# A decoder layer on one core: attention rounds written out, context products dealt unevenly over them, weight scaling moved ahead

## The chip, the core and the metric

One core of a Trainium2 chip runs the whole program. The metric is the device time of one execution in microseconds; the median of three runs is given. Matmuls run on PE (TensorE); DVE is VectorE, ACT is ScalarE, POOL is GpSimd, and SP is the engine whose queue issues nearly all DMAs.

## What is computed

The reference is one decoder layer on x of shape (16, 256, 512), cut here to its three steps:

```python
x = x + attn(layernorm(x))       # 16 heads of 32, causal softmax, biased q, k, v, o
x = x + xattn(ctx, ctx, layernorm(x), ssm_kernel, D, 8)
                                 # kv = k_i * v_j products, causal convolution with ssm_kernel, plus D*kv, times q
x = x + ffn(layernorm(x))        # rows of w_gate_up, w_down, x and h rounded to 255 levels of their maximum
```

Two preparations don't depend on x: the products kv of the context with itself (here called **context products**), and the rounding of the FFN weights by the largest magnitude of each row.

## The kernel before

**Two phases.** `attention` (L234) works through 16 batches in 16 rounds; `mixer` (L1006) then does the second and third step in rounds of its own. Engines run their own instruction streams in program order and meet at semaphores, so an engine that waits holds up everything behind the wait.

**A round** i is `body(i, p)` on every engine: 16 steps, one head each. PE at step s (L708) computes the scores of head s (L661), turns the probabilities of head s-2 (L670), does the round's share of the twelve `ROUND` jobs (L77), then multiplies the probabilities of head s-3 by the values (L685 to L687). The jobs are: projections of the next batch (QK at steps 0 to 7, V at 8 to 11), turning of the last batch's attention (A at 8 and 10) and of a normalised input (X at 12 and 13), and the output projection (O at 13 to 15). They share three PSUM banks: a job may begin once the job three before it is emptied. A job's bank is emptied by ACT one step after the job's last step (`high`, the fp16 part; for A it is L759), and then by DVE (`low`, the remainder; for A it is L882). ACT at step s (L823): such emptying, `prob_high` of head s-2 (L788), `exps` of head s (L780). DVE at step s (L963): every fourth step `divide` (L928, L932), then `maxima` of head s (L915), emptying, `prob_low` of head s-2 (L921), and at step 8 `row_stats` of batch i+2 (L897, L903). Rounds 0, 1, 14 and 15 are written out; rounds 2 to 13 are a hardware loop of two rounds an iteration (L733 on PE, L848, L989, L576, L484), six iterations.

**Context products.** 64 sets, four a round. A set is loaded by SP into one of two `c_in`, multiplied by POOL (`pairs`: L532 and L534, counted by `kv_made`), copied to fp16 by ACT (`pairs_high`, L794, counted by `kv_high`), its remainder is taken by POOL (`pairs_low`, L539, counted by `kv_low`), and SP stores it (`store_pairs`, L394), which `kv_stored` tells. ACT's copies stand behind `exps` of a step:

```python
PAIRS_HIGH = (8, 12, 15, 3)      # L91: steps of the copies of sets 0, 1, 2 of this round, and of set 3 of the round before
```

POOL's order in a round (L550) is fixed: value bias of the last four heads of the batch before (L523), bias of the residual (L557), products 0, low part of the last set of the round before, value bias, `norm(i + 2)`, products 1, low part 0, value bias, products 2, low part 1, value bias, products 3, low part 2. `norm` waits for DVE's `row_stats` of step 8:

```python
pool.wait_ge(stats_done, i + 1)  # L509, first line of norm; then L510 to L516
```

**Weight units.** `Weights` (L125): eleven units of two rows of tiles each for w_gate_up and four for w_down. SP loads a unit (L163, 512 KB), DVE finds the rows' maxima (`find_maxima`, L168) and from them scale and inverse (`find_scales`, L175 and L178), and ACT scales (`scale_rows`, L187). Units 0 to 3 are done in round 15 (`UNIT_MAX`, `UNIT_SCALE`, L87), 4 to 6 between the A and O jobs behind the rounds (L1000), 7 to 10 at the start of the mixer (L1743 to L1752, L1476, L1478 and `SCALE_AT`). PE turns them in the mixer (L194); the transposition of all scales (L1289) stands behind them and ahead of the first convolution (L1202).

Of the kernel before, what the change touches and what calls it, by code (L numbers as in the profile page):

```python
# [85 lines left out]
IN_ROUND, IN_TAIL = 4, 7  # L86
UNIT_MAX = {1: 0, 4: 1, 7: 2, 10: 3}  # L87
UNIT_SCALE = {3: 0, 6: 1, 9: 2, 12: 3}
JOBS_END = [("A", 0, -1, 0, 0), ("A", 1, -1, 0, 0), ("O", 0, -1, 0, 0), ("O", 1, -1, 0, 0)]
LOOP0, LOOP1 = 2, B - 2  # L90
PAIRS_HIGH = (8, 12, 15, 3)  # L91
# [142 lines left out]
def attention(nc, ctx, x, wqT, wkT, wvT, woT, bq, bk, bv, bo, w1, W, eye, mask, x1d, eye_f, eye_b, wqkv, x_all,  # L234
# [115 lines left out]
    with nc.Block() as block:  # L350
        @block.sync
        def _(sp):
# [30 lines left out]
            def load_ctx(i, k):  # L383

                alone(sp, started)
                reached(sp, kv_made, i * 4 + k - 1)
                sp.dma_start(c_in[k % 2][:], ctxr[bass.ds(i * 2 + k // 2, 1), :, PM * (k % 2):PM * (k % 2) + PM, :]
                             .rearrange("h p m c -> p (h m) c")).then_inc(ctx_in[k % 2], 16)

            def store_pairs(i, k):  # L390

                alone(sp, started)
                sp.wait_ge(kv_low, i * 4 + k + 1)
                sp.dma_start(kvd[bass.ds(i * 4 + k, 1)].rearrange("q p c -> p (q c)"),  # L394
                             kv_s[k % 2][:].rearrange("p a m c -> p (a m c)")).then_inc(kv_stored[k % 2], 16)
# [12 lines left out]
            load_ctx(0, 0)  # L408
            load_ctx(0, 1)
# [4 lines left out]
            def body(i, p):  # L414
# [25 lines left out]
                if isinstance(i, int) and i == B - 2:  # L440
# [1425 lines left out]
```

## Time and profile before

| | |
|---|---|
| median of 3 runs | 1227.86 us (1225.43 to 1227.94) |
| the profiled execution | 1225.79 us, of which the span of the instructions is 1224.0 us |
| busy share of the span: PE, DVE, ACT, POOL | 93%, 82%, 72%, 77% |
| attention rounds 2 to 13, by PE's scores of head 0 | 108.34 to 537.11 us |
| rounds 14 and 15 | 537.11 to 570.45 to 608.66 us |

All times below are counted from the first instruction. A round is cut where PE starts the scores of head 0. A row of a timeline reads: start, duration, engine, line, operation, output<-inputs, shapes, count, and in brackets the idle time of the engine before it with what ended it. "PEclk" is the granted TensorE clock as a share of 2.4 GHz; 0.50 is 1.2 GHz.

### The profile page before, as it was taken

How to read it: one execution, taken by the hardware profiler on the slowest of the kernel's cores; microseconds unless marked ns; L12 is line 12 of the kernel's file. 1: busy time of each engine (PE TensorE's matmuls, PEld its weight loads, DVE VectorE, ACT ScalarE, POOL GpSimd, SP SyncE). 2: the span in 40 equal slices, each digit the busy share in tenths (PEclk: the TensorE clock that was granted, in tenths of full speed). 3: DMA queues.
4: the chain of work that ended last, by engine and by line, in shares of the span. 5: the costliest groups of instructions: out<-in, count | busy, mean ns of one | idle time of the engine just before them, and what ended most of it. 6: DMA issues, size and time to landing. Idle time of an engine off the chain costs nothing. (4 is left out here: it accounts for less than half of the span.)

```text
span 1224.0 us, 33638 instructions
## 1 busy us (share of the span) xinstructions
PE 1133.6 (93%) x10114; PEld 815.9 (67%) x10114; DVE 1002.3 (82%) x3147; ACT 880.0 (72%) x1811; POOL 946.3 (77%) x1085
## 2 busy tenths in 40 slices
PE   8989999999999999998768899999999999999996
PEld 6767777778777787776446566666666666666662
DVE  5678888878787887887768788988889888898875
ACT  3778888878788887887746566667666676666764
POOL 1377786767778776877635799999999999999983
PEclk9989999999999999998679999999999999999999
DMA  7355555556655555666675434444334443344410
GB/s 215 96 168 182 170 173 166 185 173 193 181 166 169 167 175 182 194 188 194 233 242 180 146 95 132 140 146 130 109 131 140 146 131 106 131 142 145 130 35 27
DMA packets 88297, 188.28 MB, mean 154 GB/s; under 512 B 12351, under 2 KB 29017, under 8 KB 88089
## 3 DMA queue, kind: packets, MB, share of 16 engines
q1 hardware_dynamic: 87353, 186.74, 48.8%
q10 hardware_dynamic: 864, 0.66, 0.4%
q8 instruction: 28, 0.46, 0.2%
q14 instruction: 52, 0.43, 0.1%
HBM read 107.57 MB, written 54.62 MB: 133 GB/s over the span
## 5 line engine op out<-in xcount | busy, mean ns | idle before, releaser
L780 ACT ACTIVATE prob<-masked,negmax 128x128 f32<-128x128 f32 (+1 forms) x512 | 206.3, 454 | 73.2 <-DVE negmax L915 72.2
L915 DVE CUSTOM_DVE_ANT_0 masked<-s_ps,mask_f 128x128 f32<-128x128 f32 (+1 forms) x512 | 161.1, 352 | 29.3 <-PE s_ps L661 19.5
L1260 PE MATMUL f_ps<-wqkv,xiT 128*128 128x512 bf16 (+1 forms) x768 | 173.8, 363 | 2.3 <-DVE up L1717 1.4
L1543 POOL TENSOR_TENSOR tree<-prod 128x512 f32<-128x512 f32 x128 | 163.4, 1277 | 11.2 <-DVE prod L1647 11.1
L1451 ACT ACTIVATE silu<-gate,sx 128x512 f32<-128x512 f32 (+1 forms) x96 | 66.0, 687 | 135.8 <-DVE gate L1711 135.7
L539 POOL TENSOR_TENSOR kv_s<-kv_f,kv_s 128x1152 f16<-128x1152 f32 x64 | 152.3, 2380 | 4.3 <-ACT kv_s L794 4.2
L921 DVE TENSOR_TENSOR pT_lo<-t_ps,pT_hi 128x384 f16<-128x384 f32 x256 | 140.6, 550 | 16.3 <-ACT pT_hi L788 16.0
L532 POOL TENSOR_TENSOR kv_f<-c_in 128x1024 f32<-128x1024 f32 x64 | 145.9, 2280 | 1.1 <-DMA c_in<-in_ctxr 1.1
L788 ACT CAST pT_hi<-t_ps 128x384 f16<-128x384 f32 x256 | 122.4, 478 | 29.8 <-PE t_ps L670 28.6
L598 PE MATMUL g_ps<-x_all,wqkv 128*128 128x256 f16 x512 | 140.1, 274 | 2.8 <-DVE x_all L879 2.8
L600 PE MATMUL g_ps<-x_all,wqkv 128*128 128x256 f16 x512 | 140.2, 274 | 0.0
L599 PE MATMUL g_ps<-x_all,wqkv 128*128 128x256 f16 x512 | 140.2, 274 | 0.0
L670 PE MATMUL t_ps<-eye_f,prob 128*128 128x128 f32 x768 | 131.0, 280 | 0.0
L1260 PEld LDWEIGHTS f_ps<-wqkv,xiT 128*128 128x128 bf16 x768 | 74.8, 98 | 71.8 <-DVE up L1717 2.9
L1565 POOL TENSOR_TENSOR hid<-silu,up 128x512 f32<-128x512 f32 (+1 forms) x96 | 113.8, 1185 | 10.2 <-DVE up L1717 4.0
L1635 DVE TENSOR_TENSOR prod<-y_ps,qT 128x512 f32<-128x512 f32 x128 | 87.0, 680 | 35.7 <-PE y_ps L1204 34.3
L685 PE MATMUL o_ps<-v_hi,pT_hi 128*128 128x33 f16 x768 | 85.8, 180 | 30.0 <-DVE pT_lo L921 23.8
L523 POOL TENSOR_TENSOR att<-att,bv_b 128x128 f32<-128x128 f32 x128 | 55.8, 457 | 74.3 <-DVE att L932 74.3
L685 PEld LDWEIGHTS o_ps<-v_hi,pT_hi 128*128 128x128 f16 x768 | 68.0, 97 | 56.8 <-DVE pT_lo L921 36.1
L1545 POOL TENSOR_TENSOR tree<-tree 128x256 f32<-128x256 f32 x128 | 93.6, 732 | 10.0
L670 PEld LDWEIGHTS t_ps<-eye_f,prob 128*128 128x128 f32 x768 | 95.3, 145 | 0.1
L1202 PE MATMUL y_ps<-kv,x_all 128*128 128x288 f16 x320 | 92.3, 288 | 1.5 <-DVE x_all L1729 1.5
(187 smaller groups left out, 3597.8 us busy)
## 6 DMA issues: line engine op xcount, KB each, us to landing
kv_pairs<-kv_s SPq DMA_DIRECT2D x64, 576.0 KB, 3.4
kv<-kv_pairs SPq DMA_DIRECT2D x32, 1152.0 KB, 8.1
c_in<-in_ctxr SPq DMA_DIRECT2D x64, 192.0 KB, 2.5
q_st<-w_raw SPq DMA_DIRECT2D x192, 64.0 KB, 2.0
k_st<-w_raw SPq DMA_DIRECT2D x192, 64.0 KB, 2.0
x_all<-in_x SPq DMA_DIRECT2D x16, 512.0 KB, 6.5
x_res<-in_x SPq DMA_DIRECT2D x16, 512.0 KB, 5.9
x_after_attention<-x_out SPq DMA_DIRECT2D x16, 512.0 KB, 4.4
```

The source lines that it names most:

```text
L532: nc.gpsimd.tensor_tensor(f[:, :, 0:4 * w].rearrange("p m (d c) -> p m d c", d=4), c[:, :, None, 0:w].broadcast_to([P, PM, 4, w]), shifted ...
L539: nc.gpsimd.tensor_tensor(kv_s[k % 2][:, 1], kv_f[k % 2][:], kv_s[k % 2][:, 0], ALU.subtract).then_inc(kv_low, 1)
L598: nc.tensor.matmul(dst, ah, bh, start=t == 0, stop=False)
L599: nc.tensor.matmul(dst, ah, bl, start=False, stop=False)
L600: mm = nc.tensor.matmul(dst, al, bh, start=False, stop=t == DT - 1)
L670: mm = nc.tensor.transpose(t_ps[h % 2][:, c * P:(c + 1) * P], prob[h % 2][:, c * P:(c + 1) * P], eye_f[:])
L685: nc.tensor.matmul(dst, ph, v_hi[p][:, kt, head, 0:VW], start=kt == 0, stop=False)
L780: ins = nc.scalar.activation(prob[h % 2][:, at:at + w], masked[h % 2][:, at:at + w], ACT.Exp, bias=negmax[:, h % 2, t:t + 1], scale=-1.0)
L915: ins = nc.vector.tensor_tensor_reduce(masked[h % 2][:, at:at + w], s_ps[h % 2][:, at:at + w], mask_f[:, S - w:S], -1.0, FAR, ALU.add, ALU ...
L921: nc.vector.tensor_tensor(pT_lo[h % 2][:], t_ps[h % 2][:, 0:PCOL], pT_hi[h % 2][:], ALU.subtract).then_inc(plo_done, 1)
L1260: mm = nc.tensor.matmul(f_ps[side][:, 0:w], xiT[:, t, :], w1T[:, t, side * I_FF + at:side * I_FF + at + w], start=t == 0, stop=t == DT - 1)
L1543: nc.gpsimd.tensor_tensor(tree4[:], pr[:, :, 0:4 * w], pr[:, :, 4 * w:8 * w], ALU.add).then_inc(t4_done, 1)
```

## The change

All engines' `Fori` loops over rounds 2 to 13 become Python loops, so that each round is its own code and waits on constants. Sets are numbered through (q); rounds 3, 6, 9 and 12 have five sets, round 15 has none, the others four. Copies of the sets stand at new steps in five-set rounds. Seven units are found and scaled in rounds 13, 14 and 15 (two, two, three) instead of four in round 15; units 7 to 9 come behind the rounds, and only unit 10 is left to the mixer. SP's order follows. Left out of the diff: renamed arguments, and the same loop edit for each engine.

```diff
-UNIT_SCALE = {3: 0, 6: 1, 9: 2, 12: 3}
+IN_ROUND, IN_TAIL = 7, 10
+UNIT_MAX = {(B - 3, 4): 0, (B - 3, 10): 1, (B - 2, 4): 2, (B - 2, 10): 3, (B - 1, 3): 4, (B - 1, 7): 5, (B - 1, 11): 6}
+UNIT_SCALE = {(B - 3, 6): 0, (B - 3, 12): 1, (B - 2, 6): 2, (B - 2, 12): 3, (B - 1, 5): 4, (B - 1, 9): 5, (B - 1, 13): 6}
 JOBS_END = [("A", 0, -1, 0, 0), ("A", 1, -1, 0, 0), ("O", 0, -1, 0, 0), ("O", 1, -1, 0, 0)]
 LOOP0, LOOP1 = 2, B - 2
-PAIRS_HIGH = (8, 12, 15, 3)
+FIVE = (3, 6, 9, 12)
+PAIRS_HIGH = {4: (8, 12, 15), 5: (4, 8, 11, 14)}
+def pair_sets(i):
+    return 0 if i == B - 1 else 5 if i in FIVE else 4
+def pairs_before(i):
+    return sum(pair_sets(k) for k in range(i))
...
-                if not first:
-                    load_ctx(i, 1)
-                    store_pairs(i - 1, 2)
-                load_ctx(i, 2)
-                if not first:
-                    store_pairs(i - 1, 3)
+                n, q = pair_sets(i), pairs_before(i)
+                if not first and not last:
+                    load_ctx(q + 1)
+                    store_pairs(q - 2)
+                if not last:
+                    load_ctx(q + 2)
+                if not first and not last:
+                    store_pairs(q - 1)
                 if has(jobs, "QK"):
                     k = 1 + max(n for n, j in enumerate(jobs) if j[0] == "QK")
-                    if not isinstance(i, int):
-                        sp.lower_val((i + 1) * (6 * 16))
-                    alone(sp, started)
                     sp.wait_ge(g_free, jobs_before(i) + k)
                     stack(i + 1, 1 - p, 0)
                     stack(i + 1, 1 - p, 1)
-                if isinstance(i, int) and i == B - 2:
+                if not last:
+                    load_ctx(q + 3)
+                    store_pairs(q)
+                if has(jobs, "QK"):
+                    stack(i + 1, 1 - p, 2)
+                if n == 5:
+                    load_ctx(q + 4)
+                    store_pairs(q + 1)
+                if i < B - 2:
+                    load_ctx(q + n)
+                if has(jobs, "QK"):
+                    stack(i + 1, 1 - p, 3)
+                if not last:
+                    store_pairs(q + n - 3)
+                if i == B - 4:
                     sp.wait_ge(w_split, split_after(3))
                     W.load(sp, 0, w1)
                     W.load(sp, 1, w1)
-                if last:
+                if i == B - 3:
+                    W.load(sp, 2, w1)
+                    W.load(sp, 3, w1)
+                if i == B - 2:
                     for j in range(HPT):
                         sp.wait_ge(stacked[j], (B - 1) * (6 * 16))
                     W.load(sp, 4, w1)
+                if last:
                     W.load(sp, 5, w1)
-                load_ctx(i, 3)
-                store_pairs(i, 0)
-                if has(jobs, "QK"):
-                    stack(i + 1, 1 - p, 2)
-                if last:
                     for j in range(HPT):
                         sp.wait_ge(stacked[j], B * (6 * 16))
                     W.load(sp, 6, w1)
                     W.load(sp, 7, w1)
-                if not last:
-                    load_ctx(i + 1, 0)
-                if has(jobs, "QK"):
-                    stack(i + 1, 1 - p, 3)
-                store_pairs(i, 1)
-                if isinstance(i, int) and i == B - 2:
-                    W.load(sp, 2, w1)
-                if last:
                     sp.wait_ge(g_free, jobs_before(B - 1))
-                    for u in (8, 9, 10):
+                    for u in (8, 9):
                         W.load(sp, u, w1)
+                    store_pairs(NQ - 2)
+                    store_pairs(NQ - 1)
+                    W.load(sp, 10, w1)
                 if has(jobs, "O"):
                     store(i - 1, jobs_before(i) + len(jobs))
                 residual(i)
-                if isinstance(i, int) and i == B - 2:
-                    W.load(sp, 3, w1)
...
-            with sp.Fori(LOOP0, LOOP1 - 1, 2) as i:
+            for i in range(LOOP0, LOOP1, 2):
...
-            store_pairs(B - 1, 2)
-            store_pairs(B - 1, 3)
...
             def body(i, p):
-                jobs = round_jobs(i)
-                first = isinstance(i, int) and i == 0
-                if has(jobs, "O"):
-                    value_bias(i - 1, 1 - p, HPT - 1)
+                jobs, n, q = round_jobs(i), pair_sets(i), pairs_before(i)
+                def biased_residual():
                     pool.wait_ge(res_loaded, i * 16)
                     nc.gpsimd.tensor_tensor(x_res[:], x_res[:], bo_b[:, None, :].broadcast_to([P, TT, D]),
                                             ALU.add).then_inc(res_biased, 1)
-                pairs(i, 0)
-                if not first:
-                    pairs_low(i - 1, 3)
+                if has(jobs, "O"):
+                    value_bias(i - 1, 1 - p, HPT - 1)
+                if n == 0:
+                    value_bias(i, p, 0)
+                    pairs_low(q - 1)
+                    biased_residual()
+                    value_bias(i, p, 1)
+                    value_bias(i, p, 2)
+                    return
+                if has(jobs, "O"):
+                    biased_residual()
+                pairs(q)
+                if i > 0:
+                    pairs_low(q - 1)
                 value_bias(i, p, 0)
                 if has(jobs, "X"):
                     norm(i + 2)
-                pairs(i, 1)
-                pairs_low(i, 0)
+                pairs(q + 1)
+                pairs_low(q)
+                if n == 5:
+                    pairs(q + 2)
                 value_bias(i, p, 1)
-                pairs(i, 2)
-                pairs_low(i, 1)
+                if n == 5:
+                    pairs_low(q + 1)
+                pairs(q + n - 2)
+                pairs_low(q + n - 3)
                 value_bias(i, p, 2)
-                pairs(i, 3)
-                pairs_low(i, 2)
+                pairs(q + n - 1)
+                pairs_low(q + n - 2)
...
-            pairs_low(B - 1, 3)
...
-            def pairs_high(i, k):
-                act.wait_ge(kv_made, i * 4 + k + 1)
-                reached(act, kv_stored[k % 2], 16 * (i * 2 + k // 2))
-                nc.scalar.copy(kv_s[k % 2][:, 0], kv_f[k % 2][:]).then_inc(kv_high, 1)
+            def pairs_high(q):
+                act.wait_ge(kv_made, q + 1)
+                reached(act, kv_stored[q % 2], 16 * (q // 2))
+                nc.scalar.copy(kv_s[q % 2][:, 0], kv_f[q % 2][:]).then_inc(kv_high, 1)
...
-                    if s == PAIRS_HIGH[3] and not (isinstance(i, int) and i == 0):
-                        pairs_high(i - 1, 3)
-                    for k in range(3):
-                        if s == PAIRS_HIGH[k]:
-                            pairs_high(i, k)
+                    if (i, s) in UNIT_SCALE:
+                        W.scale_rows(act, UNIT_SCALE[i, s])
+                    if s == 3 and i > 0:
+                        pairs_high(pairs_before(i) - 1)
+                    for k in range(pair_sets(i) - 1):
+                        if s == PAIRS_HIGH[pair_sets(i)][k]:
+                            pairs_high(pairs_before(i) + k)
...
-                    if isinstance(i, int) and i == B - 1 and s - 1 in UNIT_MAX:
-                        W.find_scales(dve, UNIT_MAX[s - 1])
-                    if isinstance(i, int) and i == B - 1 and s in UNIT_MAX:
-                        W.find_maxima(dve, UNIT_MAX[s])
+                    if (i, s - 1) in UNIT_MAX:
+                        W.find_scales(dve, UNIT_MAX[i, s - 1])
+                    if (i, s) in UNIT_MAX:
+                        W.find_maxima(dve, UNIT_MAX[i, s])
...
-    MAX_AT, SCALE_AT = {1: N_W1, 3: N_W1 + 1, 5: N_W1 + 2, 7: N_W1 + 3}, {1: 9, 2: 10, 3: N_W1, 4: N_W1 + 1, 6: N_W1 + 2, 8: N_W1 + 3}
+    MAX_AT, SCALE_AT = {1: N_W1, 3: N_W1 + 1, 5: N_W1 + 2, 7: N_W1 + 3}, {1: IN_TAIL, 3: N_W1, 4: N_W1 + 1, 6: N_W1 + 2, 8: N_W1 + 3}
...
-            W.scale_rows(act, 7)
             take(1)
-            W.scale_rows(act, 8)
             take(3)
             take(5)
...
-            for u in (7, 8):
-                W.find_maxima(dve, u)
-                W.find_scales(dve, u)
             ln_stats(0, 0)
             aggregate(0, st2, st2_done, mv2, mv2_done)
             take(2)
             take(4)
-            for u in (9, 10):
-                W.find_maxima(dve, u)
-                W.find_scales(dve, u)
+            W.find_maxima(dve, IN_TAIL)
+            W.find_scales(dve, IN_TAIL)
             take(6)
```

## Rows read from the trace of the kernel before

**Rows 1.** The page: busy time and share; PE's granted clock in 40 slices.
```profile
PE 1133.6 (93%) x10114; PEld 815.9 (67%) x10114; DVE 1002.3 (82%) x3147; ACT 880.0 (72%) x1811; POOL 946.3 (77%) x1085
...
PEclk9989999999999999998679999999999999999999
```

**Rows 2.** Windows (length, busy PE, PEld, DVE, ACT, POOL; PEclk, DMA): rounds 2-13, 12, 13, 14, 15.
```profile
108.34:537.11 428.77, 416.25 (x4615) 322.77 (x4611) 350.88 (x1346) 354.69 (x817) 322.01 (x301) 1.00 0.57 177
...
465.41:502.12 36.71, 35.01 (x392) 26.72 (x388) 29.06 (x113) 29.27 (x69) 26.82 (x26) 1.00 0.55 172
502.12:537.11 34.99, 34.45 (x390) 27.02 (x387) 29.39 (x114) 29.77 (x69) 26.82 (x26) 1.00 0.59 180
537.11:570.45 33.34, 33.34 (x384) 26.25 (x379) 26.81 (x108) 27.70 (x65) 25.52 (x21) 1.00 0.65 208
570.45:608.66 38.21, 24.62 (x246) 18.25 (x243) 29.03 (x101) 27.14 (x59) 24.12 (x19) 0.64 0.69 232
```

**Rows 3.** DVE's loop line, 250 to 254 us, and its timeline behind the branch.
```profile
L989 DVEq COMPARE_BRANCH  x1: 68/68/68, 250.3 to 250.3; - x1
L989 DVEq FUSED_REGOPS  x1: 74/74/74, 253.2 to 253.2; - x1
...
253.48 0.29 DVE L915 CUSTOM_DVE_ANT_0 masked<-s_ps,mask_f 128x128 f32<-128x128 f32 x1 [2.12 <-PE s_ps L661]
```

**Rows 4.** Timeline of round 13, POOL.
```profile
515.70 2.38 POOL L539 TENSOR_TENSOR kv_s<-kv_f,kv_s 128x1152 f16<-128x1152 f32 x1
...
522.93 0.20 POOL L510 TENSOR_TENSOR var_e<-mv,eps 128x2 f32<-128x2 f32 x1 [4.02 <-DVE mv L903]
...
526.96 2.39 POOL L539 TENSOR_TENSOR kv_s<-kv_f,kv_s 128x1152 f16<-128x1152 f32 x1
```

**Rows 5.** Timeline of round 13, ACT: steps 5, 7, 8, 9 and 12.
```profile
513.29 0.47 ACT L788 CAST pT_hi<-t_ps 128x384 f16<-128x384 f32 x1
...
518.41 0.80 ACT L780 ACTIVATE prob<-masked,negmax 128x128 f32<-128x128 f32 x2 [0.91 <-DVE negmax L915]
...
520.89 1.15 ACT L794 CAST kv_s<-kv_f 128x1152 f16<-128x1152 f32 x1
521.93 0.59 ACT L759 CAST aT_hi<-g_ps 128x512 f16<-128x512 f32 x1
...
530.37 1.15 ACT L794 CAST kv_s<-kv_f 128x1152 f16<-128x1152 f32 x1
```

**Rows 6.** Timeline of round 13, DVE and PE, around step 10.
```profile
523.43 0.69 DVE L882 TENSOR_TENSOR aT_lo<-g_ps,aT_hi 128x512 f16<-128x512 f32 x1
...
524.18 0.39 PE L598 MATMUL g_ps<-wqkv,x_all 128*128 128x512 f16 x1 [0.26 <-DVE aT_lo L882]
```

**Rows 7.** Timeline of round 15, PE, around a gap.
```profile
596.51 0.49 PE L670 MATMUL t_ps<-eye_f,prob 128*128 128x128 f32 x3
599.91 0.19 PE L685 MATMUL o_ps<-v_hi,pT_hi 128*128 128x33 f16 x1 [2.91 <-DVE att L932]
...
600.44 0.85 PE L670 MATMUL t_ps<-eye_f,prob 128*128 128x128 f32 x3
```

**Rows 8.** Timeline of round 15: DVE's scale of two units, POOL beside the second.
```profile
585.88 0.16 DVE L175 TENSOR_SCALAR w_scale<-w_max 128x2 f32<-128x2 f32 x1
591.94 2.21 DVE L175 TENSOR_SCALAR w_scale<-w_max 128x2 f32<-128x2 f32 x1
...
591.76 2.37 POOL L539 TENSOR_TENSOR kv_s<-kv_f,kv_s 128x1152 f16<-128x1152 f32 x1
```

**Rows 9.** Timeline, ACT and DVE, from the end of round 14 on.
```profile
572.97 1.15 ACT L794 CAST kv_s<-kv_f 128x1152 f16<-128x1152 f32 x1 [2.23 <-DMA kv_pairs<-kv_s]
...
580.50 1.32 ACT L187 ACTIVATE w_raw<-w_raw,w_inv 128x512 f32<-128x512 f32 x2
...
583.26 0.56 DVE L921 TENSOR_TENSOR pT_lo<-t_ps,pT_hi 128x384 f16<-128x384 f32 x1 [2.40 <-ACT pT_hi L788]
583.74 1.21 DVE L168 TENSOR_REDUCE w_max<-w_raw 128x2 f32<-128x1024 f32 x1
```

More of the change, by code:

```diff
@@ L407, in _ @@
             sp.dma_start(tap_d[:], dvec.rearrange("a h -> h a"), allow_slow_non_contiguous=True).then_inc(taps_in, 16)
-            load_ctx(0, 0)
-            load_ctx(0, 1)
+            load_ctx(0)
+            load_ctx(1)
             sp.wait_ge(g_free, 1 + max(n for n, j in enumerate(JOBS0) if j[0] == "QK"))
@@ L524, in value_bias, with pairs @@
                 ins.then_inc(attb_done, 1)
-            def pairs(i, k):
-                q, c, f, w = i * 4 + k, c_in[k % 2], kv_f[k % 2], HJ * HB
-                pool.wait_ge(ctx_in[k % 2], 16 * (i * 2 + k // 2 + 1))
+            def pairs(q):
+                c, f, w = c_in[q % 2], kv_f[q % 2], HJ * HB
+                pool.wait_ge(ctx_in[q % 2], 16 * (q // 2 + 1))
                 reached(pool, kv_low, q - 1)
@@ L534, in pairs, with pairs_low @@
                 nc.gpsimd.tensor_tensor(f[:, :, 4 * w:], c[:, :, 0:w // 2], c[:, :, w // 2:w], ALU.mult).then_inc(kv_made, 1)
-            def pairs_low(i, k):
-                pool.wait_ge(kv_high, i * 4 + k + 1)
-                nc.gpsimd.tensor_tensor(kv_s[k % 2][:, 1], kv_f[k % 2][:], kv_s[k % 2][:, 0], ALU.subtract).then_inc(kv_low, 1)
+            def pairs_low(q):
+                pool.wait_ge(kv_high, q + 1)
+                nc.gpsimd.tensor_tensor(kv_s[q % 2][:, 1], kv_f[q % 2][:], kv_s[q % 2][:, 0], ALU.subtract).then_inc(kv_low, 1)
             norm(0)
@@ L564, in body @@
                     norm(i + 2)
-                pairs(i, 1)
-                pairs_low(i, 0)
+                pairs(q + 1)
+                pairs_low(q)
+                if n == 5:
+                    pairs(q + 2)
                 value_bias(i, p, 1)
-                pairs(i, 2)
-                pairs_low(i, 1)
+                if n == 5:
+                    pairs_low(q + 1)
+                pairs(q + n - 2)
+                pairs_low(q + n - 3)
                 value_bias(i, p, 2)
-                pairs(i, 3)
-                pairs_low(i, 2)
+                pairs(q + n - 1)
+                pairs_low(q + n - 2)
             for i in range(LOOP0):
                 body(i, i % 2)
-            with pool.Fori(LOOP0, LOOP1 - 1, 2) as i:
+            for i in range(LOOP0, LOOP1, 2):
                 body(i, 0)
@@ L732, in _ @@
                 body(i, i % 2)
-            with pe.Fori(LOOP0, LOOP1 - 1, 2) as i:
+            for i in range(LOOP0, LOOP1, 2):
                 body(i, 0)
@@ L837, in body @@
                         normalise(i + 2, x_before(i))
-                    if isinstance(i, int) and i == B - 1 and s in UNIT_SCALE:
-                        W.scale_rows(act, UNIT_SCALE[s])
-                    if s == PAIRS_HIGH[3] and not (isinstance(i, int) and i == 0):
-                        pairs_high(i - 1, 3)
-                    for k in range(3):
-                        if s == PAIRS_HIGH[k]:
-                            pairs_high(i, k)
+                    if (i, s) in UNIT_SCALE:
[5 more added lines that the diff above has]
+                            pairs_high(pairs_before(i) + k)
             for i in range(LOOP0):
                 body(i, i % 2)
-            with act.Fori(LOOP0, LOOP1 - 1, 2) as i:
+            for i in range(LOOP0, LOOP1, 2):
                 body(i, 0)
@@ L854, in _ @@
                 prob_high((B - 1) * H + s - 2, s - 2)
-            pairs_high(B - 1, 3)
             n0 = jobs_before(B)
@@ L981, in body @@
                         row_stats(i + 2)
-                    if isinstance(i, int) and i == B - 1 and s - 1 in UNIT_MAX:
-                        W.find_scales(dve, UNIT_MAX[s - 1])
-                    if isinstance(i, int) and i == B - 1 and s in UNIT_MAX:
-                        W.find_maxima(dve, UNIT_MAX[s])
+                    if (i, s - 1) in UNIT_MAX:
+                        W.find_scales(dve, UNIT_MAX[i, s - 1])
+                    if (i, s) in UNIT_MAX:
+                        W.find_maxima(dve, UNIT_MAX[i, s])
             for i in range(LOOP0):
                 body(i, i % 2)
-            with dve.Fori(LOOP0, LOOP1 - 1, 2) as i:
+            for i in range(LOOP0, LOOP1, 2):
                 body(i, 0)
```

18 lines of the change are left out of this document (8 added, 10 removed).

## The prediction

> **What bounds the kernel now.** I read the page first: PE is busy 93% of the span, and its clock is full except in slices 1 to 3 and around the middle of the span [rows 1]. Then the windows by round: in round 13 PE is busy 34.45 of 34.99 us, in round 14 all of 33.34 us, so these rounds are PE's. Round 12, the first of a loop iteration, takes 36.71 us, and in round 15 PE is busy 24.62 of 38.21 us at a clock of 0.64 [rows 2]. So there are two places to gain: the loop, and round 15 with what follows it. Last I read the timeline of round 13 for what ACT and POOL do when, since the change gives four such rounds more of it.
>
> **The loop.** DVE's branch ends at 250.4 us and its next instruction starts at 253.2; DVE idles 2.12 us for it [rows 3]. A first round costs 36.71 - 34.99 = 1.72 us more than a second [rows 2]. Five branches are taken behind round 2, so 8.6 us; the same from the whole: 428.77 - 12 x 34.99 = 8.9 us [rows 2]. I take -8.8, between -7 and -9. Register arithmetic for waits goes too; it is worth nothing while PE is busy 34.45 of 34.99 us. That straight code could be fetched late is bounded by round 14, which is written out already and has no idle PE [rows 2]: 0. The Trainium skill (Runtime: NRT & Kernel Launch, Instruction fetch mechanics) says that a taken branch outside the fetched window stalls while straight code streams; by it all engines' branches would stall, and the sum would be the same, since PE's loss is counted whole.
>
> **Five-set rounds.** Here is the largest term. Steps of round 13 stand for steps of rounds 3, 6, 9 and 12 with the loop gone. The order of POOL ahead of the second set is unchanged, but ACT now asks for the sets earlier.
> First set, copied at step 4. ACT is through step 4 at 513.29 [rows 5], when its next head begins; POOL has the products at 515.70, where L539 starts [rows 4]. ACT waits 2.4 us and copies for 1.04 (520.89 to 521.93 [rows 5]), so all behind it is 3.5 us later. There is slack: 0.91 us before `exps` of step 7 [rows 5], some at DVE. But `divide` at step 7 waits for the values of head 3, whose probabilities are behind the copy, and `maxima` stand behind it. Following head 3 through PE, DVE and ACT I get `exps` of step 7 at 521.2 instead of 518.41, so 2.8 us remain.
> Second set, copied at step 8, where before the first was. ACT arrives at 520.89 [rows 5]. POOL makes this set only after `norm(i + 2)`, which waited 4.02 us for DVE's `row_stats` of the same step 8 and began at 522.93; the products are there at 526.96 [rows 4]. ACT stands 6.1 us at a wait that before came at 530.37 [rows 5], 3.4 us after the products. Behind it are queued A's emptying (521.93 [rows 5]), `prob_high` of head 7 and `exps` of head 9. PE runs on until step 10, where V's second job needs A's bank: it started at 524.18, just after DVE's L882 of 523.43 [rows 6]. ACT is free at 526.96 + 1.04 = 528.0, its L759 takes 0.59 [rows 5], so L882 starts at 528.6 instead of 523.43 and PE starts 5.2 us late. The third and fourth set (steps 11, 14) find POOL ahead: a low part takes it 2.38 us and the products at most the 4.0 us from 522.93 to 526.96 [rows 4], and ACT is late by then.
> Together 5.2 + 2.8 = 8.0 us. PE's gap is then about 6.5 us. Around the gap of 2.91 us at 599.91 the same three transposes took 0.49 us before and 0.85 after, at the lower clock of 1.2 GHz [rows 7]; some 3 us of PE's work at half speed costs 1.2 more. I take 9 us a round, 36 in all. Bounds: 5.2 (the first wait wholly absorbed, no clock loss), so 21; and 3.5 + 6.1 + 2 = 11.6, so 46. The next round takes the late POOL work without loss: POOL idles 4.02 us at `norm` [rows 4] and as much at value biases.
>
> **Units in rounds 13 and 14.** Two units a round: DVE 1.21 us for L168, 0.16 for L175 and about as much for L178, so 1.5 each [rows 8, 9]; ACT 1.32 each for L187 [rows 9]. DVE goes from 29.4 and 26.8 busy to 32.4 and 29.8, ACT from 29.8 and 27.7 to 32.4 and 30.3 [rows 2]. PE covers this on average but not at steps 10 to 12 of round 13, where it already waits for DVE [rows 6]. L175 took 0.16 us, but 2.21 when POOL's L539 had started just before it, ending with it [rows 8], and POOL is busy 77% of these rounds [rows 2]. I take 1 us a unit, 4 in all, between 1 and 9. The Trainium skill (SBUF — State Buffer, Who interferes with whom) says that a VectorE op in a two-port mode and a GpSimd op shut each other out for a whole instruction; by it each of the four L175 could lose 2.2 us, and the sum would be 5 higher than mine.
> SP: units 0 to 3 (512 KB each) move from round 14 to the ends of rounds 12 and 13, ahead of the residual's load. If POOL gets the residual 3 us later, its first products come at 518.7 instead of 515.70 [rows 4], still ahead of ACT's step 8 at 520.89 [rows 5]: 0. In round 14 the store that ACT waited 2.23 us for [rows 9] stood behind units 0 and 1; that wait goes, and is counted with round 15, where PE paid it.
>
> **Round 15.** ACT loses three set copies (3 x 1.04) and one unit (1.3), DVE one unit (1.5) and the long L175 (2.1 and another of some 1.5). DVE is left 29.0 - 1.5 - 3.6 = 24 us of work. PE, DVE and ACT hand heads round, so the waits count: 2.23 at the store and 2.40 where a unit and a copy met on ACT [rows 9], the latter several times. I add 5 us of waits to 24: 29, so 9 us less, between 5 and 12. Late next is the clock, still at 0.5 for much of the round, and DVE.
> **Behind it.** The last low part no longer stands before POOL's value bias: between 0 and 2.4 us (one L539), I take 0.8. Units 7, 8, 9 take the place of 4, 5, 6 between A and O: 0. In the mixer three units go; the two before the first x_ln hide behind its load, unit 9 is ahead of the scales' transposition and the first convolution: 1.5 us, between 0 and 3.
>
> **Sum.** -8.8 + 36 + 4 - 9 - 0.8 - 1.5 = +19.9 us. Against the profiled execution's 1225.8 that is 1245.7; the median of the runs is 2 us above that execution, within their spread. I say 1246. Its own range, with the bounds mixed, is 1238 to 1257.
>
> **Rivals.**
> A, the waits are absorbed: PE's queued work and the slack of steps 9 to 13 swallow ACT's stop, and a five-set round costs little more than a copy. Price 4 x 0.5 = 2 in place of 36: 1225.8 - 8.8 + 2 + 4 - 11.3 = 1211.7, faster. It decides at step 10: PE must not be reached by the wait for L882, so the second products must be there before about 521.5 on round 13's axis. For it: ACT is busy only 29.77 of 34.99 us, and POOL 26.82 [rows 2], so on average there is room. Against it: engines wait in program order, and 526.96 is given by `norm`. Chance 0.15.
> B, one wait only: POOL or PE slack takes the first stop, the clock holds. 4 x 5.2 = 20.8, so 1225.8 - 8.8 + 20.8 + 4 - 11.3 = 1230.5, 0.2% over the median. The 0.91 us idle of ACT [rows 5] speaks for part of it. Chance 0.20.
> C, worse: each stop keeps its full length, half clock lasts into steps 13 to 15, L175 blocks at each unit: 4 x 11 + 8 = 52 in place of 40, so 1258. Round 15's clock, at 0.64 on average [rows 2], shows that it can stay low. Chance 0.12.
> D, the change doesn't shorten round 15: PE, with less beside it, stays at the low clock and the hand-over of heads sets the pace. With the rest as forecast, 1246 + 9 = 1255. The clock of 0.64 speaks for it, the 24 us left to DVE against it. Chance 0.03.
> My forecast has 0.50.
>
> **How the numbers follow.** Below 1226 lie A and the low end of B: near 0.17; above 1260 some 0.04. The range is 1226 to 1260. A difference of 0.2%, 2.5 us, is about what can be told from no change. Faster: A and a little of B, 0.17. Same (1225.4 to 1230.3): a third of B, 0.08. Slower: the forecast, C and the rest of B, 0.75.
>
> **What would show it.** In the windows by round: 35.0 us for 2, 4, 5, 7, 8, 10, 11; about 44 for 3, 6, 9, 12; 36 to 38 for 13; 34 to 36 for 14; about 29 for 15. In ACT's waits a line L794 <- POOL kv_f L534 of about 8.5 us a five-set round, 6 of them at step 8, which before had none in these rounds; PE gaps of 5 us or more and a clock below 1 four times between 140 and 540 us; DVE's gap behind a branch gone from rounds 2 to 13. I am wrong if PE has no gap over 2 us in round 3: then A holds. If only the step 8 wait shows, B. If written-out rounds take over 35.5 us, the fetch costs what I set at 0.

## The result and the profile after

The changed kernel takes 1257.12 us (median of 4 runs, 1254.75 to 1261.45), the kernel before took 1226.64 in the same comparison (4 runs). The ratio on record is 1.0263, 95% interval [1.0239, 1.0287] (the two medians alone give 1.025): slower. The forecast of 1246 had the side and the largest mechanism right and was 11 us short. The profiled execution took 1254.84 us.

The page of the changed kernel: busy time and share, the granted clock in 40 slices, and the group of ACT's set copies (busy us, mean ns | idle just before them, and what ended it).

```profile
PE 1137.5 (91%) x10114; PEld 815.5 (65%) x10114; DVE 1001.1 (80%) x3147; ACT 884.9 (71%) x1811; POOL 946.8 (76%) x1085
...
PEclk9989989999999999899889999999999999999999
...
L821 ACT CAST kv_s<-kv_f 128x1152 f16<-128x1152 f32 x64 | 73.1, 1142 | 38.8 <-POOL kv_f L547 38.6
```

No engine has more work than before; PE's 4 us of extra busy time [rows 1] are the same matmuls, more of them at a lower clock. ACT now idles 38.6 us in front of its copies, for POOL's products. The dip of the clock around the middle of the span is shallower. Of the five-set rounds only the first shows in the slices (the 8 at 157 us), and the two 8s behind the middle lie in the mixer, so the clock is better read from the windows below.

The windows by round, from PE's first scores of one round to those of the next: rounds 2, 3, 4, 6, 9, 12, 13, 14, 15 (columns as in [rows 2]).

```profile
107.48:142.41 34.93, 34.46 (x392) 27.04 (x388) 29.29 (x114) 29.85 (x69) 26.87 (x26) 1.00 0.60 189
142.41:187.60 45.19, 37.63 (x391) 28.41 (x388) 29.55 (x114) 31.98 (x71) 31.91 (x29) 0.92 0.52 163
187.60:222.66 35.06, 34.46 (x391) 27.00 (x388) 29.14 (x114) 28.93 (x68) 26.92 (x26) 1.00 0.55 174
257.58:303.63 46.05, 37.65 (x391) 28.34 (x387) 29.55 (x114) 31.99 (x71) 31.92 (x29) 0.93 0.50 159
373.75:421.52 47.77, 38.32 (x392) 28.82 (x387) 29.50 (x114) 32.25 (x71) 31.87 (x29) 0.89 0.51 158
491.38:537.36 45.98, 37.43 (x392) 27.98 (x387) 29.41 (x114) 32.38 (x71) 31.90 (x29) 0.93 0.52 163
537.36:575.00 37.64, 35.12 (x391) 26.79 (x387) 32.14 (x119) 31.22 (x71) 26.68 (x25) 1.00 0.60 192
575.00:612.40 37.40, 33.91 (x384) 26.05 (x379) 31.68 (x113) 30.11 (x70) 25.70 (x23) 1.00 0.68 216
612.40:643.77 31.37, 21.76 (x247) 15.76 (x243) 24.84 (x99) 24.38 (x57) 12.26 (x12) 0.78 0.60 214
```

A four-set round of the old loop is 34.93 to 35.2 us, a first one among them. The five-set rounds are 10.3, 11.1, 12.8 and 11.1 us above 34.93, together 45.3. The clock column is 0.89 to 0.93 in these four and 1.00 in the four-set rounds. Rounds 2 to 12 take 429.88 us (107.48 to 537.36) where the same eleven took 393.78 [rows 2], +36.1; so the loop gave back 9.2. Round 13 adds 2.7 and round 14 4.1 us; round 15 gives 6.8, and what follows it 6.1 (1253.0 - 643.77 = 609.2 against 1224.0 - 608.66 = 615.3 us). With 0.9 us less ahead of round 2 that is the +29.0 us of the two spans.

Where the round's 10 us go is seen in round 3. First ACT's timeline (start, duration, in brackets the idle time before and its releaser):

```profile
156.69 1.15 ACT L821 CAST kv_s<-kv_f 128x1152 f16<-128x1152 f32 x1 [3.01 <-POOL kv_f L547]
...
170.86 1.15 ACT L821 CAST kv_s<-kv_f 128x1152 f16<-128x1152 f32 x1 [6.02 <-POOL kv_f L547]
```

POOL's timeline of the same stretch:

```profile
166.77 0.20 POOL L523 TENSOR_TENSOR var_e<-mv,eps 128x2 f32<-128x2 f32 x1 [4.17 <-DVE mv L929]
...
168.19 2.23 POOL L545 TENSOR_TENSOR kv_f<-c_in 128x1024 f32<-128x1024 f32 x1
170.37 0.45 POOL L547 TENSOR_TENSOR kv_f<-c_in 128x128 f32<-128x128 f32 x1
```

And PE's:

```profile
158.87 0.19 PE L712 MATMUL o_ps<-v_hi,pT_hi 128*128 128x33 f16 x1 [2.32 <-DVE pT_lo L947]
...
159.27 0.76 PE L697 MATMUL t_ps<-eye_f,prob 128*128 128x128 f32 x3
...
162.87 0.49 PE L697 MATMUL t_ps<-eye_f,prob 128*128 128x128 f32 x3
...
173.28 0.61 PE L625 MATMUL g_ps<-wqkv,x_all 128*128 128x512 f16 x1 [5.01 <-DVE aT_lo L908]
...
176.74 0.38 PE L625 MATMUL g_ps<-wqkv,x_all 128*128 128x512 f16 x1
```

ACT stands 3 us at step 4 and 6 us at step 8. At step 8 POOL itself had stood 4.17 us for DVE's row statistics before it normed and multiplied; the wait is the chain that the prediction named. Each stop opens a gap in PE (2.32 and 5.01 us), and behind **each** of them PE runs at the lower clock, 1.2 GHz, for a stretch: the three transposes take 0.76 us at 159.27 and 0.49 at 162.87, a projection matmul 0.61 at 173.28 and 0.38 at 176.74. The granted clock is 0.56 from 158.9 to 162.7 us and 0.50 from 173.3 to 176.4; between and behind them it is 1.00.

### The profile page after: what moved, and what is told of

It is laid out like the page before. It is cut to its first block and busy times, and to the rows that moved or that the text cites. A ratio compares the mean times of both kernels' runs of the same rounds, so it can differ in the third digit from the quotient of the medians.

```text
span 1253.0 us, 32052 instructions
## 1 busy us (share of the span) xinstructions
PE 1137.5 (91%) x10114; PEld 815.5 (65%) x10114; DVE 1001.1 (80%) x3147; ACT 884.9 (71%) x1811; POOL 946.8 (76%) x1085
## 5 line engine op out<-in xcount | busy, mean ns | idle before, releaser
L815 ACT CAST pT_hi<-t_ps 128x384 f16<-128x384 f32 x256 | 122.4, 478 | 35.7 <-PE t_ps L697 34.5
L821 ACT CAST kv_s<-kv_f 128x1152 f16<-128x1152 f32 x64 | 73.1, 1142 | 38.8 <-POOL kv_f L547 38.6
```

## Experiments

Each text of expectations was set down before its run. Ratios are to the kernel before, on the same chip. Round lengths run from PE's first scores to the next round's, as in the windows. Line numbers of the variants are close to those of the changed kernel (its 821 is ACT's copy, 547 and 545 POOL's products, 568 the residual's bias, 178 DVE's maxima).

**The loop alone.** The kernel before, its five `Fori` written out, nothing else.

```diff
-            with sp.Fori(LOOP0, LOOP1 - 1, 2) as i:
+            for i in range(LOOP0, LOOP1, 2):
```

> The kernel before with its loops over rounds 2 to 13 written out and nothing else changed. The theory (a taken branch costs PE 1.7 us through DVE, straight code costs nothing): rounds 2 to 13 take 12 x 34.99 = 419.9 us instead of 428.8, the whole is 8.9 us below the kernel before, about 1217. The rival (straight code is fetched late somewhere): rounds of 35.5 us and more, the whole 1223 or above.

Measured 1217.6 us (10 runs), ratio 0.9933 [0.9912, 0.9954]: by the ratio 8.2 us less. The windows of rounds 2 to 12, 14 and 15 (round 13 takes 34.93 us):

```profile
106.29:490.90 384.61, 379.16 (x4230) 297.18 (x4227) 321.97 (x1234) 328.10 (x749) 295.34 (x276) 1.00 0.59 183
...
525.83:559.16 33.33, 33.33 (x382) 26.23 (x379) 26.81 (x108) 27.71 (x65) 25.55 (x21) 1.00 0.71 222
559.16:598.81 39.65, 24.38 (x247) 17.49 (x244) 30.85 (x102) 27.56 (x60) 24.85 (x19) 0.66 0.64 213
```

384.61 / 11 = 34.96 us a round, with the same busy time on every engine as a second round before [rows 2]. The loop's term stands, and straight code cost nothing. This is the lowest ratio of the study, though the intervals of two variants below overlap its own.

**The fifth set without the early copies.** The changed kernel with one line different: in five-set rounds ACT copies at steps 8, 12, 14 and 16.

```diff
-PAIRS_HIGH = {4: (8, 12, 15), 5: (4, 8, 11, 14)}
+PAIRS_HIGH = {4: (8, 12, 15), 5: (8, 12, 14, 16)}
```

> The changed kernel with the copies of a five-set round at steps 8, 12, 14 and 16 instead of 4, 8, 11 and 14; POOL's order and all else stay. The theory (the five-set rounds are long because ACT stands at sets that POOL has not made): five-set rounds of 36 to 38 us instead of 45 to 48, the whole near 1254.8 - 4 x 8.5 = 1221. The rival (a fifth set is more work for POOL and ACT than a round holds, wherever the copies stand): five-set rounds stay over 42 us and the whole over 1245.

Measured 1219.91 us, ratio 0.9962 [0.9943, 0.998]. The five-set round 3, the round 4 behind it, and rounds 13, 14, 15:

```profile
145.59:180.51 34.92, 34.45 (x390) 27.02 (x387) 29.27 (x114) 30.89 (x70) 27.44 (x24) 1.00 0.59 183
180.51:216.83 36.32, 35.00 (x392) 26.74 (x388) 28.98 (x114) 29.50 (x69) 31.20 (x31) 1.00 0.59 187
498.92:539.64 40.72, 35.71 (x391) 26.49 (x388) 33.19 (x119) 31.84 (x72) 31.00 (x30) 1.00 0.62 198
539.64:577.90 38.26, 34.08 (x383) 25.97 (x380) 31.11 (x113) 29.94 (x70) 25.64 (x23) 1.00 0.69 217
577.90:610.23 32.33, 24.02 (x247) 17.70 (x243) 24.85 (x99) 24.62 (x57) 12.27 (x12) 0.68 0.60 209
```

A round with a fifth set, its copies at steps that POOL can serve, takes 34.92 us (36 to 38 were expected). The whole excess of the five-set rounds was in the **steps** at which ACT asks, not in the work. Part of the fifth set's work on POOL falls into the next round (POOL busy 31.20 us there), which costs 1.4, 0.8 and 1.9 us in rounds 4, 7 and 10. But rounds 13 and 14 now take 5.8 and 4.9 us more than in the kernel with the loop alone, worse than in the changed kernel.

**The two stops apart.** The copies at (4, 12, 14, 16), and at (7, 8, 11, 14).

```diff
+PAIRS_HIGH = {4: (8, 12, 15), 5: (4, 12, 14, 16)}    # first stop only
+PAIRS_HIGH = {4: (8, 12, 15), 5: (7, 8, 11, 14)}     # second stop only
```

> The changed kernel with copies at steps 4, 12, 14 and 16: the early request of the first set stays, that of the second goes. If the two waits cost PE separately as I worked out, PE has a gap of 2 to 4 us at step 6 and none at step 10, and a five-set round takes 35 + 3 + 1 for the clock = 38 to 40 us; the whole about 1227 to 1232. If the first wait is absorbed (rival B) it takes under 37 us and the whole is as copies_late.

> The changed kernel with copies at steps 7, 8, 11 and 14: the first set is there in time, the second is asked for as early as in the change. PE has no gap at step 6 and one of about 5 us at step 10; a five-set round takes 35 + 5.2 + 1.5 for the clock = about 41.7 us, the whole about 1254.8 - 4 x 4.5 = 1237. If the second wait is not what costs (say, the third and fourth sets do), the rounds fall under 39 us.

One run each: 1234.5 and 1241.24 us, 2.5 and some 4 us above what was expected; the rounds came out as expected or 1 us longer. Round 3 with the first stop only (columns as before):

```profile
141.59:181.04 39.45, 36.13 (x392) 28.02 (x388) 29.25 (x114) 30.87 (x70) 27.44 (x24) 0.96 0.54 169
```

and with the second only, and its first gap of PE:

```profile
141.45:184.15 42.70, 36.05 (x392) 27.72 (x388) 29.54 (x114) 32.16 (x71) 31.90 (x29) 0.92 0.54 172
```

```profile
169.84 0.61 PE L625 MATMUL g_ps<-wqkv,x_all 128*128 128x512 f16 x1 [6.58 <-DVE aT_lo L908]
```

The first stop alone costs 3.5 to 4.6 us a round (39.45, 39.53, 38.46, 38.82 against 34.93), the second alone 7.8 each time. PE's idle part in round 3 (length less busy, less the 0.47 that a quiet round has) is 2.9 and 6.2 us, its busy part 1.7 and 1.6 us above 34.46: one half-clock stretch for each stop. With the first stop only, round 4 too has a gap (2.27 us) and takes 38.48 us, where it takes 36.32 with late copies. ACT's waits are 3.0 to 4.1 and 6.02 us, where the working had 2.4 and 6.1. Together in the changed kernel the two lose about 11.3, a little less than the sum of the two, 4.1 + 7.8 = 11.9.

**Curing the second stop at its source.** The changed kernel, but in five-set rounds POOL makes the second set ahead of `norm(i + 2)`.

```diff
+                if n == 5:
+                    pairs(q + 1)
                 if has(jobs, "X"):
                     norm(i + 2)
-                pairs(q + 1)
+                if n == 4:
+                    pairs(q + 1)
```

> The changed kernel, copies at its own steps 4, 8, 11 and 14, but in five-set rounds POOL makes the second set's products ahead of norm instead of behind it. The theory (the second wait is 6.0 us because these products stand behind norm, which waits for DVE's step 8): ACT's wait at step 8 falls from 6.0 us to under 1, the one at step 4 stays at 3 to 5, PE has no gap over 1 us at step 10, five-set rounds take 38 to 40 us and the whole about 1227 to 1231. If it is the early step alone, whatever POOL's order, the wait and the rounds stay as they are.

One run: 1262.89 us; five-set rounds 46.76, 46.81, 48.2, 47.24. What ACT's copies waited for in all, and the third copy of round 3:

```profile
  DMA kv_pairs<-kv_s: 19.0, 4
  POOL kv_f L547: 17.4, 7
```

```profile
177.15 1.15 ACT L824 CAST kv_s<-kv_f 128x1152 f16<-128x1152 f32 x1 [4.99 <-DMA kv_pairs<-kv_s]
```

The wait at step 8 fell from 6.02 to 0.43 us, so it was indeed the place behind `norm` that made it. But the third copy then stood 4.1 to 5.2 us for the **store** of the set two before it, whose buffer it needs; that store stands behind the next round's first stacks in SP's order. In the changed kernel the 6 us at step 8 had hidden it. So here a set that was ready early didn't help. The expectation (1227 to 1231) was missed; the combination with SP's order changed wasn't tried, so that it would help is not shown.

**Units: work or loads?** The kernel with late copies, with the unit work (DVE and ACT) back where the kernel before has it (four in round 15, the rest in the mixer), while SP loads units 0 to 3 early, as in the change.

```diff
-UNIT_MAX = {(B - 3, 4): 0, (B - 3, 10): 1, (B - 2, 4): 2, (B - 2, 10): 3, (B - 1, 3): 4, (B - 1, 7): 5, (B - 1, 11): 6}
+UNIT_MAX = {(B - 1, 1): 0, (B - 1, 4): 1, (B - 1, 7): 2, (B - 1, 10): 3}
...
```

> copies_late (copies of five-set rounds at steps 8, 12, 14, 16) with the weight units where the kernel before has them: 0 to 3 in round 15, 4 to 6 behind the rounds, 7 to 10 in the mixer; the loads stay early. It tells what the moved units cost. From copies_late's own rounds: round 13 falls from 40.7 to 35-36 us, round 14 from 38.3 to 33.4, together 10 us; given back are one unit and its waits in round 15 (1.5 to 3) and 1.5 us in the mixer, so the whole about 1214. If the units' early place is a gain on balance, it comes out above 1220.

Measured 1224.92 us, ratio 1.0004 [0.9985, 1.0023]. Rounds 13 and 14, and the waits in them (engine, line waited for: us in total, times, longest):

```profile
499.49:537.76 38.27, 34.97 (x392) 26.75 (x388) 28.98 (x114) 29.53 (x69) 30.65 (x30) 1.00 0.62 197
537.76:576.95 39.19, 35.30 (x383) 26.79 (x380) 26.67 (x108) 27.88 (x65) 25.99 (x23) 0.96 0.68 216
```

```profile
POOL x_res L568 <- DMA x_res<-in_x: 16.6, 2, 9.2
DVE aT_lo L908 <- ACT aT_hi L786: 7.4, 3, 4.7
...
ACT kv_s L821 <- DMA kv_pairs<-kv_s: 6.0, 3, 3.8
```

DVE does no unit in these rounds (28.98 and 26.67 us busy, as before [rows 2]), and still they are 3.3 and 5.9 us longer; 35 to 36 and 33.4 us were expected, and 1214 us for the whole. Not all of round 13's 3.3 is the loads': in this kernel rounds 4, 7 and 10, behind a five-set round but with no unit loaded, take 1.3, 2.6 and 1.4 us more than a quiet one. POOL waits 16.6 us for the residual's two loads. In round 13 its first products are late by that, ACT stands 2.55 us for them at step 8 and PE 2.19 us. In round 14 ACT stands 3.84 us for a store that SP issued behind the two units, `x_out`, the residual and a load of 1152 KB, and PE stands 3.51 us. So with late copies the step that I had put at 0 is not 0.

The residual is late for two reasons. SP issues it later: 8.48 us into round 13 here and 8.66 in the kernel with late copies, 3.15 in the kernel before and 1.62 in the changed kernel. Behind the other five-set rounds of the kernel with late copies, with no unit on the way, it is 7.0 to 8.0 us, so most of this comes with the late copies and their stores. And it takes longer from issue to landing. The store of `x_out` and the load of the residual, rounds 13 and 14, median us of that time in the kernel with the loop alone:

```profile
x_after_attention<-x_out SPq DMA_DIRECT2D x2, 512.0 KB, 4.3
x_res<-in_x SPq DMA_DIRECT2D x2, 512.0 KB, 5.9
```

and with late copies and early loads:

```profile
x_after_attention<-x_out SPq DMA_DIRECT2D x2, 512.0 KB, 7.8
x_res<-in_x SPq DMA_DIRECT2D x2, 512.0 KB, 8.8
```

The residual lands 2.9 us later from its own issue; in rounds 4 and 5 of the kernel with late copies the same load takes 6.7 us. The Trainium skill (DMA: Bandwidth & Descriptors, Two DMAs through the same engine are not ordered) says that within one queue of one DMA engine descriptors start in order; the trace agrees, the residual landing behind the two units issued ahead of it.

**Other places for the units.** Five further kernels move the loads or the work. All have the late copies.

```diff
 # units_early: maxima at steps 2 and 5, scaled at 4 and 7 of rounds 13 and 14
+UNIT_MAX = {(B - 3, 2): 0, (B - 3, 5): 1, (B - 2, 2): 2, (B - 2, 5): 3, ...
 # copies_next_round: the same, and the last two copies of a five-set round at steps 1 and 5 of the next
+                    if i - 1 in FIVE and s == 1:
+                        pairs_high(pairs_before(i) - 2)
 # loads_mid: units loaded in the middle of rounds 12 and 13, between stacks
 # loads_mid_next: loads_mid with copies_next_round's copies and steps
 # loads_behind: units loaded behind residual(i) at the ends of rounds 12 and 13
+                if i in (B - 4, B - 3):
+                    for u in (0, 1):
+                        W.load(sp, 2 * (i - B + 4) + u, w1)
```

> copies_late with the units of rounds 13 and 14 found at steps 2 and 5 and scaled at 4 and 7 instead of 4, 10 and 6, 12: away from steps 9 to 13, where PE already waits for DVE. If the cost is the place, rounds 13 and 14 fall from 40.7 and 38.3 to 36-37 and 34-36 us, the whole to about 1214. If it is the work itself or VectorE's blocked L185 at any step, they stay over 39 and 37.

> units_early with the fourth copy of a five-set round at step 1 and the fifth at step 5 of the round behind it. In copies_late ACT waited eight times, 8.0 us in all, for stores of earlier sets, and rounds 4, 7 and 10 took 36.3, 35.7 and 36.8 us. The theory: these waits go, rounds 4, 7 and 10 fall to 35.0, the whole 3 us below units_early, about 1211. If they come back elsewhere, the two are the same.

> copies_late with the loads of units 0 to 3 taken from the ends of rounds 12 and 13, where they stand ahead of the residual's load, into the middles of these rounds (one behind the stacks of step 8, one behind the third stack). Theory: rounds 13 and 14 of copies_late (40.7 and 38.3 us against 34.9 and 33.3 without the change) are long because the residual lands late behind 1 MB of units, POOL makes the first sets late, and ACT waits; of 10.7 us some 6 to 9 are this. Then POOL's waits for x_res in rounds 13 and 14 fall under 2 us, the two rounds to 37 and 35, the whole to about 1213. Rival: the units' own work on DVE and ACT is the cost; the rounds stay within 1 us, the whole at 1220.

> loads_mid with the copies of copies_next_round (8, 12, 14, then steps 1 and 5 of the round behind) and the units at steps 2 and 5, which now have their data in time. In units_early DVE waited 4.35 and 2.93 us for a unit's load at these steps; that goes. If steps 9 to 13 are the wrong place for units, rounds 13 and 14 take 35 to 36.5 and 34 to 35 us and the whole 1209 to 1211; if the place is indifferent, it equals loads_mid.

> copies_late with the same loads put behind the residual's load at the ends of rounds 12 and 13. The residual is in time (POOL's waits for x_res under 2 us), but the first stores and context loads of the next round now stand behind 1 MB. If the residual alone was the cost, the result is that of loads_mid; if any 1 MB at a round's end delays something, rounds 13 and 14 stay above 38 and 36 us, with ACT's L821 waiting for stores.

| kernel | us | ratio [95%] | rounds 13, 14, 15 | longest new wait |
|---|---|---|---|---|
| units_early | 1229.54 | 1.005 [1.003, 1.0071] | 44.82, 40.56, 33.56 | DVE for a unit's load, 4.4 us |
| copies_next_round | 1227.3 | 1.0033 [1.0016, 1.005] | 45.26, 40.99, 31.21 | the same, 5.2 us |
| loads_mid | 1226.4 | 1.0013 [0.9992, 1.0035] | 45.93, 36.79, 30.69 | ACT for a store, 6.0 us |
| loads_mid_next | 1222.58 | 0.998 [0.9962, 0.9997] | 42.54, 39.36, 32.87 | ACT for a store, 3.1 us |
| loads_behind | 1220.11 | 0.9955 [0.9929, 0.998] | 40.96, 39.09, 29.58 | ACT for a store, 2.5 us |

None reached the 35 us of a quiet round 13, and the 1209 to 1214 us that the theories of the first four give were missed by 11 us and more. Wherever two units are loaded in a round, something waits: behind the residual, ACT for a store (2.5 us) and DVE for a unit (0.8); ahead of it, POOL; in mid-round, ACT for the store behind them, though POOL's waits for the residual are down to 1.4 us; asked for too early, DVE. The waits for transfers add up to less than the rounds' excess, and every one of these kernels also does the unit work on DVE there; the five runs don't part the two. The copies moved into the next round bring rounds 4, 7 and 10 to 35.6 to 35.8.

**One unit at a time.** Late copies; unit 0 to 3 loaded behind the residual of rounds 1, 4, 7 and 10, and found and scaled in the round after.

```diff
+UNIT_MAX = {(2, 4): 0, (5, 4): 1, (8, 4): 2, (11, 4): 3, (B - 1, 3): 4, (B - 1, 7): 5, (B - 1, 11): 6}
+UNIT_SCALE = {(2, 6): 0, (5, 6): 1, (8, 6): 2, (11, 6): 3, (B - 1, 5): 4, (B - 1, 9): 5, (B - 1, 13): 6}
...
+                if i in (1, 4, 7, 10):
+                    W.load(sp, i // 3, w1)
```

> copies_late (1219.91 us) with the four units loaded one at a time behind the residual of rounds 1, 4, 7 and 10, and each found and scaled in the quiet round after it (2, 5, 8, 11), none in rounds 12 to 14. Theory (two units at once, 2 MB of loads within two rounds that also store and load the residual, make the waits of rounds 13 and 14; one unit in a round that has no fifth set is covered): rounds 13 and 14 fall from 40.72 and 38.26 us to 35 to 36.5 and about 33.5, rounds 2, 5, 8 and 11 rise by at most 1.5 us each from 35, round 15 stays at 29 to 32: 1211 to 1215 us, below unroll_only (1217.6). Rival (a unit costs 2 us or more in whatever round it is loaded and scaled): rounds 2, 5, 8, 11 rise by 2 to 2.5 us each, what rounds 13 and 14 give back is spent, and the time is 1218 to 1222 us.

Measured 1222.38 us (12 runs), ratio 0.9994 [0.9975, 1.0013]. Rounds 2, 8, 13 and 14 (5 takes 38.10 and 11 takes 36.15 us), and what DVE waited for in round 2:

```profile
111.37:149.49 38.12, 34.81 (x392) 26.87 (x388) 30.90 (x117) 30.99 (x71) 26.86 (x26) 1.00 0.59 187
...
329.47:365.99 36.52, 34.81 (x390) 26.88 (x387) 31.00 (x117) 30.90 (x71) 26.86 (x26) 1.00 0.62 197
...
508.02:543.61 35.59, 34.78 (x392) 26.89 (x388) 28.98 (x114) 29.59 (x69) 31.18 (x31) 1.00 0.59 187
543.61:576.95 33.34, 33.34 (x383) 26.26 (x379) 26.76 (x108) 27.79 (x65) 25.60 (x22) 1.00 0.68 215
```

```profile
DVE w_max L178 <- DMA w_raw<-in_w: 1.7, 1, 1.7
```

Rounds 13 and 14 did fall to 35.59 and 33.34 us, as the theory had it, which ties their length to the units, work and loads together. But rounds 2, 5, 8 and 11 pay 3.2, 3.2, 1.6 and 1.2 us, 9.2 together, where rounds 13 and 14 give 10.1: the rival's arithmetic, and the time lies above the rival's own range. Round 15, at 34.22 us, is 1.9 longer than with late copies. In rounds 2 and 5 DVE stood 1.7 and 1.6 us for the load; the maxima at a later step might save about that, which wasn't tried. Even covered on average, a unit costs 1.2 us or more of a round whose PE is busy 34.5 of 34.9 us.

## Why the prediction was right or wrong

**Right: the side and the place.** The time, 1257.1, lies in the range of 1226 to 1260, at the upper end of the narrower 1238 to 1257 that the terms' bounds gave. Rivals A (waits absorbed) and B (one wait only) fell: PE had both gaps, at the named instructions. ACT's second wait is 6.02 us in each of four rounds against the 6.1 read from before, its first 3.01, 3.87, 4.83 and 2.82 us against 2.4. D fell too: round 15 is shorter. C, which had 0.12, came nearest in number: it put five-set rounds and units at 44 + 8 = 52 us, and they measured 45.3 + 6.7 = 52.0. Its first part held, the stops kept nearly their full length, and two of four `find_scales` were blocked for 0.9 us or more; but the low clock did not last into steps 13 to 15, it was back at 1.00 within 4 us of each gap in round 3. So the forecast's side was right with a sum for these two terms that was 12 us short.

**The five-set term: 36 forecast, 45.3 measured.** This is the mis-sized one. It splits into PE's idle and its slower clock. Idle is 7.56, 8.40, 9.45 and 8.55 us in the four windows, less 0.47 that a quiet round has: 8.0 on average, and 8.0 was the forecast. Busy is 37.63, 37.65, 38.32 and 37.43 us against 34.46: 3.3 us on average, where the working had 1.2 (and took only 1 of it). Failed step: "some 3 us of PE's work at half speed costs 1.2 more". It counted one stretch behind the long gap; there are two, for the first stop's 2.32 us gap does it as well. The runs with one stop alone price them at 1.7 and 1.6 us. That the idle came out at 8.0 holds an error that cancelled, so that match is partly luck: the second stop alone left PE idle 6.2 us where the working had 5.2 (the first 2.9, as the 2.8 forecast), and together they left less than their sum.

**The loop: 8.8 forecast, 9.2 here, 8.2 with the loop alone.** Right, and so was the 0 for fetching straight code. The Trainium skill (Runtime: NRT & Kernel Launch, Instruction fetch mechanics) gives the fetch behind a taken branch as one reason why kernels prefer full unrolling where possible; the run agrees with 8.2 us for five branches.

**Units in rounds 13 and 14: 4 forecast, 6.7 measured.** Inside its bounds of 1 to 9, and too small by 2.7. The trace of the changed kernel shows where it lies, and it isn't the loads. There the step "If POOL gets the residual 3 us later ... still ahead of ACT's step 8: 0" came out as forecast: POOL begins the residual's bias 9.64 and 12.33 us into rounds 13 and 14 (8.65 and 9.51 before), and none of ACT's copies in these rounds waits, neither for POOL nor for a store. The mis-sized step is "I take 1 us a unit"; the two rounds lost 1.7 us a unit. DVE is busy 2.8 and 4.9 us more than in [rows 2], and every gap of PE over 0.2 us in the two rounds is ended by DVE. The chain at the second unit of round 14 (`find_maxima`, `find_scales`, ACT behind the maxima of scores, PE):

```profile
599.87 1.21 DVE L178 TENSOR_REDUCE w_max<-w_raw 128x2 f32<-128x1024 f32 x1
...
603.25 1.64 DVE L185 TENSOR_SCALAR w_scale<-w_max 128x2 f32<-128x2 f32 x1
```

```profile
602.30 0.80 ACT L807 ACTIVATE prob<-masked,negmax 128x128 f32<-128x128 f32 x2 [1.40 <-DVE negmax L941]
...
605.74 0.80 ACT L807 ACTIVATE prob<-masked,negmax 128x128 f32<-128x128 f32 x2 [1.80 <-DVE negmax L941]
```

```profile
606.83 0.19 PE L712 MATMUL o_ps<-v_hi,pT_hi 128*128 128x33 f16 x1 [1.25 <-DVE pT_lo L947]
```

The changed kernel with its unit work taken out of these rounds wasn't run, so this is read from one trace and not tested. With late copies it is another case: there the two rounds were long without any unit work in them, and POOL began the residual's bias 17.4 us into round 13 instead of 9.64. `find_scales` met a POOL instruction twice in round 14:

```profile
588.65 1.07 DVE L185 TENSOR_SCALAR w_scale<-w_max 128x2 f32<-128x2 f32 x1
```

```profile
587.33 2.36 POOL L568 TENSOR_TENSOR x_res<-x_res,bo_b 128x1024 f32<-128x1024 f32 x1 [4.33 <-DMA x_res<-in_x]
...
602.62 2.24 POOL L545 TENSOR_TENSOR kv_f<-c_in 128x1024 f32<-128x1024 f32 x1
```

Both, this one and that of 603.25, end with POOL's instruction, within 0.03 us. The median of all is 0.168 us, so the two cost DVE 1.07 + 1.64 - 2 x 0.17 = 2.4 us in round 14; the two of round 13 took 0.58 and 0.36 us, 0.6 more. The rule of the Trainium skill (SBUF — State Buffer, Who interferes with whom) of an exclusive lock fits these rows. How often it hits was not forecast unit by unit, and no run isolates it.

**Round 15: 9 forecast, 6.8 measured,** within 5 to 12; 39.65 with the loop alone and 29.6 to 35.9 in the variants, so a single number for it is uncertain by more than the miss. **Behind it: 2.3 forecast, 6.1 measured.** But the same code took 615.3 us in the kernel before and 618.0 with the loop alone, and 612.1 in the variant whose mixer has all its units back. And the changed kernel's own code behind the rounds took 609.0 to 615.6 us in the variants that share it. So a share of the 6 us, perhaps all of it, isn't due to the change; how much stays open.

The sum: +29.0 measured, +19.9 forecast. Five-set rounds +9.3, units +2.7, round 15 +2.2 against it; loop -0.4, behind -3.8, ahead of round 2 -0.9.

**What the change was worth without its flaw.** The kernel with late copies keeps everything else and gains 0.4%; the loop alone gains 0.7%. So moving sets and units out of round 15 gained nothing that these runs can show: in the windows round 15 gives 7.3 us against the loop alone and what follows it 6.6, and rounds 4, 7, 10, 13 and 14 pay 14.

## What to carry to other kernels

Where an engine that works in program order takes over a copy, look at the step at which its input exists and not at its free time: the same fifth set cost its round 0 us when the copies began at step 8 (and the next round 0.8 to 1.9), and 11 us with copies at steps 4 and 8. Price a gap of the matmul engine with the slow stretch that follows it, here some 1.6 us behind gaps of 2 to 3 us as behind those of 5 to 6.6. When a transfer is moved, follow everything behind it on its queue, stores that free a buffer first of all; and a wait that is removed may only uncover the store that it hid.

## What was not expected of the hardware

- A gap of 2.32 us in PE was enough to bring the lower clock for a stretch (0.76 against 0.49 us for three transposes); before, it was seen behind one of 2.91 us [rows 7].
- The longer gap cost no more of it: with one stop alone PE's busy time rose 1.7 us behind a gap of 3.28 us and 1.6 behind one of 6.58.
- With two 512 KB loads ahead on the queue the next 512 KB load took 8.8 us from its own issue, where it took 5.9 without them in another kernel, and the store between them 7.8 instead of 4.3.
- A `find_scales` of 0.17 us took 1.07 and 1.64 us beside a POOL instruction and ended with it.
- Twelve rounds of straight code ran at the pace of a written-out round (34.96 us against 34.99 [rows 2]).
